# W1 held as runs of four rows on each partition, and x turned in every fourth column

## The reference: what is computed

```python
w1 = W1[language_ids]                       # (10, 512, 128) -> one 512 x 128 matrix for each sequence
w2 = W2[language_ids]                       # (10, 128, 512)
h = relu(einsum('bsh,bha->bsa', x, w1) + b1[language_ids])
adapted = einsum('bsa,bah->bsh', h, w2) + b2[language_ids]
y = x + adapted
normed = (y - mean(y)) * rsqrt(var(y) + 1e-5)          # over the 512 channels
out = x + normed * gamma[language_ids] + beta[language_ids]
```

## Time and profile before

| | before |
|---|---|
| runs | 332.33, 331.82, 331.36 us; median 331.82 |
| profiled execution, its own time | 332.22 us |
| its span, first to last instruction | 330.5 us |
| granted TensorE clock, mean | 0.985 |
| busy | PE 91%, PEld 82%, DVE 95%, ACT 71%, POOL 57% |
| moved by DMA | 75.63 MB, 229 GB/s in the mean |

### The profile page before, as it was taken

How to read it: one execution, slowest core, us unless ns; L and a number is a source line. 1 busy time by engine, 2 the same in 40 slices (tenths; PEclk the granted TensorE clock), 3 DMA queues, 4 the chain that set the end, 5 groups by cost and what they waited for, 6 DMA issues and landing times. The chain is left out here.

```text
span 330.5 us, 8120 instructions
## 1 busy us (share of the span) xinstructions
PE 299.9 (91%) x2196; PEld 270.7 (82%) x2196; DVE 312.7 (95%) x685; ACT 234.4 (71%) x594; POOL 189.1 (57%) x217
## 2 busy tenths in 40 slices
PE   1774899999999999999999999999999999999651
PEld 1264799999999999999999999999999999999430
DVE  5859979999999999999999999999999999999996
ACT  3931477778777778777777777777777777877542
POOL 1049755665555666555666555665555666555563
PEclk9998999999999999999999999999999999999987
DMA  6999934687776677666677766677766677533234
GB/s 172 305 380 418 388 136 159 227 257 236 222 241 230 224 251 254 227 224 231 226 248 238 246 220 233 229 242 243 240 223 237 229 233 257 193 127 129 97 116 170
DMA packets 41678, 75.63 MB, mean 229 GB/s; under 512 B 2250, under 2 KB 7401, under 8 KB 41509
## 3 DMA queue, kind: packets, MB, share of 16 engines
q1 hardware_dynamic: 41571, 75.04, 67.4%
q10 hardware_dynamic: 66, 0.08, 0.1%
HBM read 41.56 MB, written 33.55 MB: 227 GB/s over the span
## 5 line engine op out<-in xcount | busy, mean ns | idle before, releaser
L265 POOL TENSOR_TENSOR x_io<-x_io,beta_all 128x512 f32<-128x512 f32 x128 | 161.6, 1284 | 0.2 <-issue 0.2
L355 PE MATMUL ps_h<-w_all,x_T 128*128 x1024 | 143.0, 283 | 0.0
L355 PEld LDWEIGHTS ps_h<-w_all,x_T 128*128 128x128 f32 x1024 | 125.5, 193 | 1.6
L309 ACT ACTIVATE cut<-ps_y,row_sum 128x512 bf16<-128x512 f32 x128 | 87.9, 687 | 26.2 <-PE ps_y L378 26.2
L293 ACT COPY x_T<-ps_T 128x512 f32<-128x512 f32 x128 | 73.8, 577 | 28.6 <-PE ps_T L347 28.6
L494 DVE SCALAR_TENSOR_TENSOR ps_y<-ps_y,mean,gamma_all 128x512 f32<-128x512 f32 x128 | 90.6, 754 | 2.4 <-ACT cut L309 2.1
L507 DVE SCALAR_TENSOR_TENSOR x_io<-ps_y,rstd,x_io 128x512 f32<-128x512 f32 x128 | 90.2, 747 | 2.7 <-DVE rstd L499 0.3
L347 PE MATMUL ps_T<-identity,x_io 128*128 128x128 f32 x512 | 78.2, 277 | 11.0 <-DMA x_io<-in_x 11.0
L485 DVE SCALAR_TENSOR_TENSOR ps_y<-x_io,b_all 128x512 f32<-128x512 f32 x128 | 86.8, 720 | 0.0
L347 PEld LDWEIGHTS ps_T<-identity,x_io 128*128 128x128 f32 x512 | 62.8, 143 | 19.9 <-issue 11.7
L262 POOL TENSOR_TENSOR mean<-row_sum,over_h 128x2 f32<-128x2 f32 x64 | 12.5, 195 | 116.3 <-DVE ps_y L485 116.3
(11 more groups left out here) (50 smaller groups left out, 178.7 us busy)
## 6 DMA issues: line engine op xcount, KB each, us to landing
x_io<-in_x SPq DMA_DIRECT2D x64, 512.0 KB, 4.5
out<-x_io SPq DMA_DIRECT2D x63, 512.0 KB, 3.0
w_all<-in_L_cond_W SPq DMA_DIRECT2D x5, 512.0 KB, 7.4
x_io<-in_L_cond_W SPq DMA_DIRECT2D x5, 512.0 KB, 8.7
b_all<-in_L_cond_b SPq DMA_DIRECT2D x1, 2560.0 KB, 16.2
out<-x_io SPq DMA_DIRECT2D x2, 256.0 KB, 2.1
x_io<-in_L_cond_gamma SPq DMA_DIRECT2D x1, 60.0 KB
x_io<-in_L_cond_beta ACTq DMA_DIRECT2D x1, 60.0 KB
```

The costliest lines, as they stand in the source:

```text
L265: nc.gpsimd.tensor_tensor(x_slot(t), x_slot(t), of_lang(beta_all, langs[b]), ALU.add)\
L309: nc.scalar.activation(squares[:, t % 2, :], ps_y[t % Y_BANKS][:, :], ACT.Square, scale=-float(H), bias=stat(row_sum, t), accum_out=stat(s ...
L355: last = nc.tensor.matmul(part, x_T[:, t % 4, c, :], w1_all[:, bass.ds(lang, 1), c, :].rearrange("p o a -> p (o a)"), start=False, stop=(c ...
```

## The change

The load of W1 takes the 512 rows of a language as 128 runs of four: partition `p` gets rows 4p to 4p+3, which lie side by side in memory and are 2 KB, where before it got rows p, 128+p, 256+p and 384+p, four pieces of 512 bytes. Group `c` of `w1_all` now holds the rows 4p+c, and so `turn_x` takes for group `c` the columns c, c+4, c+8 and so on: 128 columns that stand 16 bytes apart, where before they stood side by side. The sum over the 512 channels is the same one, in another order. Number, order, engines and waits of all instructions are as before; the products' own operands (`x_T`, `w1_all`) keep their shapes.

```diff
             for n in range(W_CHUNKS):
                 langs = slice(n * LC, (n + 1) * LC)
-                sp.dma_start(w1_all[:, langs, :, :], w1[langs].rearrange("l (c p) a -> p l c a", p=128)).then_inc(s_w1, 16)
+                sp.dma_start(w1_all[:, langs, :, :], w1[langs].rearrange("l (p c) a -> p l c a", p=128)).then_inc(s_w1, 16)
...
                 for c in range(C):
-                    last = nc.tensor.transpose(ps_T[t % 2][:, c, :], x_io[:, t % SLOTS, c * 128:(c + 1) * 128],
+                    last = nc.tensor.transpose(ps_T[t % 2][:, c, :], x_io[:, t % SLOTS, c:H:C],
                                                identity[:, :])
```

## The result

The changed kernel takes 335.12 us in the median of four runs (335.0 to 335.56), the kernel before beside it 331.77 us: ratio 1.0102, interval 1.0085 to 1.0120. It is slower by 3.35 us, where 3.0 us less were forecast. The profiled execution took 335.09 us, its span (first to last instruction) is 333.3 us.

The account below looks back on a forecast made before the run. TensorE was taken to bound the loop and one chain from W2's first chunk the prologue. The median of 331.82 us, less 3.0 for W1's load and 0 for the turns, gave 328.8 us; 8-in-10 range 327.3 to 332.6 us.

Parts of the forecast that it names:

- What bounds the kernel: Loop: TensorE leads at 4.49 us a pair, VectorE has about 0.07 us of room; prologue: one chain of waits.
- W1's load: Prologue: 2 KB pieces let W2's chunk 0 land earlier, a gain of 2.7 to 3.15 us, taken as 3.0.
- The prologue is therefore one chain: Prologue: W2's first chunk, GpSimd's 16.34 us, the seeds, the loop; moving its head moves the kernel's end.
- The 3.96 MB that I counted behind 6.68 us: Prologue: bytes that went by until chunk 0 landed; at 400 GB/s they take 9.9 us, ending at 16.6 us.
- that holds, with 1 us to spare: Prologue: x pair 4, wanted at 31.8 us, would land near 30.6 us and not hold up TensorE.
- The turned columns: Loop, `turn_x`: 512 weight loads of x read every fourth float32; cost taken as 0, with 0.5 us for the range.
- The bound by the half clock: Loop's turns: upper bound from loads at half clock, 0.103 us more each, 48.6 us over 472 turns.
- the cover: Loop's turns: each load runs beside the matmul ahead, so it may grow some 51 ns before anything shows.
- My own price of 0.47 us for each ns beyond it: Loop's turns, 59 steps: each ns of load beyond the cover of 51 ns costs 0.47 us of kernel time.
- The rival of the outgrown cover: `turn_x` in 59 steps: strided load outgrows its cover, slower by over 1.0 us from about 200 ns; chance 0.18.

Follow-up runs that it names:

- step 8: Kernel before with only the turns' step changed, to every eighth column (32 bytes apart), mixing both sequences of a pair: 332.34 us, one execution.
- step 2: Against the kernel before, W1 loaded in 1 KB pieces and x turned in every second column of each half: 335.27 us, ratio 1.0096.

## Why the prediction was wrong

**What bounds the kernel: right for the loop, half right for the prologue.** TensorE led in the loop, and each ns on its pair was paid: 0.08 us a pair, 59 times, is the +4.85 us. With W1's load alone the gain at W2's chunk 0 was also paid out to the end. But "The prologue is therefore one chain", whose head moves the end of the kernel, is wrong: with chunk 0 moved ahead of W1 the first sum came 3.4 us earlier, and the kernel was 1.5 us slower. There are two chains, W2's and TensorE's through x pair 4; in that run the second set the start, at 43.09 us.

**W1's load: right in kind, mis-sized.** I took 3.0 us; the load alone gave 2.5 us, and in the whole change it was 1.96 us by the two profiled starts and about 1.5 by the medians. I had chunk 0 land between 14.6 and 16.6 us; it landed at 17.30 in the changed kernel and 17.14 us with the load alone, above my upper end. The 3.96 MB that I counted behind 6.68 us were right and the rate wasn't: the changed kernel moved 368 GB/s over 6.68 to 18 us, not 400, and in 6 to 8 us only 244. And "that holds, with 1 us to spare" was wrong for x pair 4: I had it land near 30.6 us, it landed at 33.8, and TensorE waited 1.49 us for it.

**The turned columns: the step that failed.** "I take 0 for it, with 0.5 us for the range." The bound by the half clock (0.103 us more a load) was far too high, and the cover was about right: at 188 ns it holds (step 8), at 198 ns and more the pair grows. What was wrong was the choice between them. I put the load inside the cover because a cover was there, without a row that said how much a stride adds. It adds 66 ns, 15 more than the 51 of the cover. My own price of 0.47 us for each ns beyond it gives 7.1 us; measured are 4.85. The spacing of the turns grew by only 8 ns, to 0.118 us, which is 8 x 472 = 3.8 us. The rest is not all in the turns: the six loads of the second product take 105.77 - 104.48 = 1.29 us, where they took 106.54 - 105.27 = 1.27. Why they grow isn't shown.

**The rival of the outgrown cover (0.18): right.** I had it slower by over 1.0 us "from a load of about 200 ns"; the load is 207. With the rival's price and the gain as I sized it the sum is 328.8 + 7.1 = 335.9 us, against 335.12 measured. That it comes so near is luck: the price is 2.2 us too high and the gain, by the medians, 1.5 us too high, and the two errors work against each other. The prediction left this case out of the range as lying "far above for nearly all of its values". That was the second mistake: the values just beyond the cover were the near ones, and they lay 3 us above the range, not 50.

**The rules of the Trainium skill.** The one on lines of 16 bytes ("SBUF — State Buffer", Door 1: The DMA port swizzle) says that each access that crosses to a new line pays a penalty, and that two hits on a line are needed for full rate. Here a step of 16 bytes does slow the load. Its condition is not what the runs show: with two numbers on each line (step 2) the load takes 204 ns against 207. The same passage lets float32 stride "for free" up to four, which I had passed over; here the step of four is not free, 207 ns against 141. The other, 512 bytes as the smallest transfer for line rate ("DMA: Bandwidth & Descriptors", Specifications), doesn't hold here: 293 and 285 GB/s with 512-byte pieces, 360 and 407 with 2 KB in the same windows.

**What stays open.** Why the durations go 204, 198, 207, 188 ns over steps 2, 3, 4 and 8. Why the start is at 40.4 us with both edits and at 39.65 with the load alone, so that the whole costs 1.1 to 1.4 us more than its parts: pair 4's place alone doesn't settle it. Why the six loads of the second product take 0.02 us more in each pair.

## What to carry to other kernels

Cover is a length, not a yes: before an edit that makes a hidden operation longer is costed at nothing, compare the longest that stays hidden with what the edit may make of it, and where no row has that, let the near side of the limit have its chance and its place in the range. Where the engine that leads has no room, a one-time gain in the prologue has to pay for every pair, here 1.5 to 2.0 us against 59 x 0.08. And when short pieces slow the loads at the start, it is worth asking first which loads are wanted next, on every chain: one chunk of W2 moved ahead cost 1.5 us, two chunks and x pair 4 together gave 1.0 us with no cost in the loop.

## What the runs showed of the hardware that was not expected

- A float32 weight load of 128 columns for a transpose lasts 141 ns in the median with the columns side by side, and 204, 198, 207 and 188 ns with 8, 12, 16 and 32 bytes from one to the next. The longest is not the widest step.
- Such a load is hidden at a spacing of 0.110 us when it lasts 188 ns; at 207 ns the spacing is 0.118 us. With most of the turns under a 512-column matmul a load with the step of 16 bytes lasts 198 ns, and the stride costs 0.03 us a pair instead of 0.08.
- Moving a transpose behind each 512-column matmul brings nothing with side-by-side columns: 4.50 us a pair against 4.49.
- W1's issues on SP take 1.65 us each with 1,024 pieces of 512 bytes and 3.18/5 = 0.64 us with 256 of 2 KB: short pieces hold up the queue's issue as well as the bytes.
